# A new order of the four engines' work in the local attention layer of an eight-layer kernel

## The reference, cut to what matters

```
for i in range(DEPTH):                                   # 6
    q, k, v = heads(shift_tokens(x) @ Wqkv[i])
    q, k = rotary(l2norm(q) * qs), rotary(l2norm(k) * ksc)
    sim  = einsum(q_window, k_window_and_the_one_before) * 8
    attn = softmax(where(mask, -max, sim))
    x = merge(attn @ v) @ Wo[i] + x
    y = layernorm(shift_tokens(x)) @ W1 + b1             # feed-forward, inner 341, gelu
    x = (a * gelu(gate)) @ W2 + b2 + x
```

## Time and profile before

| | before |
|---|---|
| runs, median of 3 | 9571.57 us (9569.17 to 9572.25) |
| profiled execution | 9542.88 us, span 9541.1 us |
| PE busy | 7287.1 us (76%) |
| DVE busy | 6764.2 us (71%) |
| ACT, POOL busy | 3257.0 (34%), 3224.7 us (34%) |
| mean granted TensorE clock | 0.853 |

### The profile page before, as it was taken

One profiled execution on the slowest core, in us unless ns is written; L12 is line 12 of the kernel. 1 busy time (PEld: TensorE's weight loads), 2 busy tenths in 40 slices (PEclk: granted clock), 3 DMA queues, 4 the chain that ended last, 5 costly groups with the idle time before them and its releaser, 6 DMA issues. The chain is left out here.

```text
span 9541.1 us, 245537 instructions
## 1 busy us (share of the span) xinstructions
PE 7287.1 (76%) x92569; PEld 4453.7 (47%) x92569; DVE 6764.2 (71%) x15000; ACT 3257.0 (34%) x5970; POOL 3224.7 (34%) x3982
## 2 busy tenths in 40 slices
PE   4888888888874826656845768888888888888887
PEld 3666666666621212223223345545455545454554
DVE  7777777777758475765485557777777777777776
ACT  2222222222243313223413334444444444444444
POOL 1333333333300000210040035555555555555553
PEclk7888888888887867656865779999999999999999
DMA  0000000000000000000000031111111111111111
GB/s 18 1 1 1 1 1 1 1 1 1 1 5 1 15 0 0 0 0 1 0 0 1 1 120 54 53 53 54 48 56 51 54 51 51 56 51 56 51 56 57
DMA packets 156976, 243.21 MB, mean 25 GB/s; under 512 B 21617, under 2 KB 136849, under 8 KB 150161
## 3 DMA queue, kind: packets, MB, share of 16 engines
q1 hardware_dynamic: 155920, 228.84, 7.8%
HBM read 187.06 MB, written 13.66 MB: 21 GB/s over the span
## 5 line engine op out<-in xcount | busy, mean ns | idle before, releaser
L2751 POOL TENSOR_TENSOR big<-big 128x512 f32<-128x512 f32 x776 | 1040.1, 1373 | 278.4 <-DMA big<-norms 270.7
L2741 POOL TENSOR_TENSOR big<-big 128x512 f32<-128x512 f32 x388 | 494.7, 1275 | 1819.8 <-DVE big L2583 1819.8
L882 POOL TENSOR_TENSOR big<-big 128x128 f32<-128x128 f32 x1024 | 518.3, 506 | 1569.7 <-DVE big L820 1567.4
L604 ACT ACTIVATE big<-big 128x128 f32<-128x128 f32 x1024 | 316.8, 309 | 1902.0 <-DVE big L778 1876.8
L1856 POOL TENSOR_TENSOR small<-big 128x480 f32<-128x480 f32 (+14 forms) x240 | 220.9, 954 | 2187.2 <-ACT big L1614 1866.5
L2158 PE MATMUL banks<-hidden,big 128*128 128x256 f32 x3104 | 828.9, 401 | 111.8 <-DVE big L2583 41.1
L514 PE MATMUL banks<-big,constants_on_chip 128*128 128x128 f32 x2048 | 533.3, 347 | 409.8 <-DVE big L811 408.2
L337 PE MATMUL banks<-big,constants_on_chip 128*128 128x512 f32 (+15 forms) x1088 | 533.5, 644 | 355.2 <-DVE big L1747 191.3
L337 PE MATMUL banks<-big,weights_even 128*128 128x512 f32 (+5 forms) x1152 | 620.5, 692 | 235.0 <-DVE big L1137 45.1
L2222 PE MATMUL banks<-big,hidden 128*32 128x512 f32 x6144 | 770.5, 600 | 4.1 <-ACT big L2473 4.1
L2201 PEld LDWEIGHTS banks<-big 32*32 32x32 f32 x49152 | 535.2, 103 | 471.8 <-issue 471.1
(11 more groups left out here) (349 smaller groups left out, 15896.3 us busy)
## 6 DMA issues: line engine op xcount, KB each, us to landing
big<-norms SPq DMA_DIRECT2D x776, 128.0 KB, 2.9
big<-qk SPq DMA_DIRECT2D x50, 512.0 KB, 4.8
big<-vo SPq DMA_DIRECT2D x25, 1024.0 KB, 5.8
weights_odd<-ffn SPq DMA_DIRECT2D x25, 537.5 KB, 4.6
hidden<-big SPq DMA_DIRECT2D x171, 64.0 KB, 12.9
hidden<-big SPq DMA_DIRECT2D x25, 256.0 KB, 3.8
hidden<-big SPq DMA_DIRECT2D x25, 255.8 KB, 4.0
big<-pairs SPq DMA_DIRECT2D x6, 1024.0 KB, 10.4
```

The costliest lines, as they stand in the source:

```text
L882: nc.gpsimd.tensor_tensor(full(u["kS"][s % 2]), full(S), by(u["ko_c"]), ALU.mult).then_inc(*e.did(("kS", s)))
L2741: self.nc.gpsimd.tensor_tensor(dst, cos, sin, ALU.add).then_inc(*e.did(("turned_pair", f, name, g)))
L2751: self.nc.gpsimd.tensor_tensor(x, x, u["norms"][:, n, g].unsqueeze(1).broadcast_to([P, 2, QTOK]), ALU.mult).then_inc(*e.did(("scaled", f, ...
```

## The change

Each of the four compute engines gets a new list of steps for a phase. On TensorE, attend(f-1,1) stands behind four projections, two values, the masks and three score windows; the second masks and windows stand between the Q projections, the values and the rest of the phase; `turn_back` moves from the middle to near the end; both `mean`s move from f=0 to f=1. On ScalarE and VectorE `exps` and `normalise` of the second half go to the next phase, behind its first square and first rotation; `exit` runs the last of them. The Gelu table is loaded once in a phase that needs it. GpSimd adds Q0 before K3 and Q3 behind `keep_last`. `entry` clears the second probability buffer and five value slots in place of `probT`, the former behind the last store to DRAM. The number of matmuls, of products and of DMAs in a turn is the same. SyncE's program is not edited.

```diff
@@ -2226,10 +2226,9 @@
     def attend(self, q, jj):
         e, pe, u = self.e, self.pe, self.u
+        pe.wait_ge(*e.after("turned", q, jj))
         if e.layer == "local":
-            kw = {"back": 1} if jj and q == QUARTERS - 1 else {}
-            pe.wait_ge(*e.after("turned", q, jj, **kw))
-            pe.wait_ge(*e.after("kept", q, jj, 3, **kw))
+            pe.wait_ge(*e.after("kept", q, jj, 3, **({"back": 1} if jj and q == QUARTERS - 1 else {})))
             if jj == 0:
                 pe.wait_ge(*e.after("added", q))
...
@@ -2361,6 +2359,10 @@
             nc.vector.tensor_copy(u["folded"][d % 2][:, c * TILE:(c + 1) * TILE], core.bank[3 + c]).then_inc(
                 *e.did(("fold", d, c)))
         e.name_last("folded", d, "vector")
+    for k in range(2 * (SUBS * QUARTERS) - 5, 2 * (SUBS * QUARTERS)):
+        nc.vector.memset(u["slots"][k % SLOTS], 0.0).then_inc(*e.did())
+    dve.wait_ge(*e.after("stored", DEPTH - 1))
+    nc.vector.memset(u["prob"][1].rearrange("p c k -> p (c k)"), 0.0).then_inc(*e.did())
...
@@ -2382,46 +2384,51 @@
     t = LocalTensor(core, e)
     with e.turns("turn", TURNS):
         for f in range(QUARTERS):
-            for g in range(3):
-                t.project(f, "K", g)
-            t.attend((f - 1) % QUARTERS, 1)
-            t.project(f, "K", 3)
+            t.project(f, "K", 0)
+            t.project(f, "K", 1)
             t.value(f, 0, 0)
             t.value(f, 0, 1)
+            t.project(f, "K", 2)
+            t.project(f, "K", 3)
+            t.score_masks(f, 0)
+            t.score(f, 0, 0)
+            t.score(f, 0, 1)
+            t.score(f, 0, 2)
+            t.attend((f - 1) % QUARTERS, 1)
+            if f == 1:
+                t.mean(0)
+            t.score(f, 0, 3)
             t.sums(f, "K")
             t.project(f, "Q", 0)
-            t.score_masks(f, 0)
-            t.score(f, 0, 0)
+            t.value(f, 0, 2)
             t.project(f, "Q", 1)
-            t.score(f, 0, 1)
-            t.turn_back(f)
             t.project(f, "Q", 2)
-            t.score(f, 0, 2)
+            t.value(f, 0, 3)
+            t.score_masks(f, 1)
+            t.score(f, 1, 0)
             t.project(f, "Q", 3)
-            t.score(f, 0, 3)
+            t.value(f, 1, 0)
             t.sums(f, "Q")
-            t.value(f, 0, 2)
-            t.value(f, 0, 3)
+            t.score(f, 1, 1)
+            t.value(f, 1, 1)
+            if f == 1:
+                t.mean(1)
+            t.value(f, 1, 2)
             if f == 1:
                 t.variance(0)
-                t.variance(1)
-            if f == 3:
-                for win in range(4):
-                    t.value(f, 1, win)
+            t.score(f, 1, 2)
             if f >= 2:
                 t.up(f - 2, 0)
-            for win in range(4):
-                if f < 3:
-                    t.value(f, 1, win)
-                if win == 0:
-                    t.score_masks(f, 1)
-                t.score(f, 1, win)
-                if f >= 2 and win in (0, 3):
-                    t.up(f - 2, 1 if win == 0 else 2)
+            t.value(f, 1, 3)
+            if f >= 2:
+                t.up(f - 2, 1)
+            t.turn_back(f)
+            t.score(f, 1, 3)
+            if f >= 2:
+                t.up(f - 2, 2)
+            if f == 1:
+                t.variance(1)
             t.attend(f, 0)
-            if f == 0:
-                t.mean(0)
-                t.mean(1)
             if f >= 2:
                 t.down(f - 2)
     e.leave()
@@ -2457,7 +2464,8 @@
     def exps(self, f, jj):
         e, act = self.e, self.act
-        act.wait_ge(*e.after("lowered", f, jj))
+        if e.layer == "local":
+            act.wait_ge(*e.after("lowered", f, jj, **({"back": 1} if jj and f == QUARTERS - 1 else {})))
...
@@ -2519,36 +2523,43 @@
     core.nc.scalar.preload_act_table_set(LN_EXP)
     with e.turns("turn", TURNS):
         for f in range(QUARTERS):
-            for g in range(GROUPS):
-                a.square(f, "K", g)
+            a.square(f, "K", 0)
+            a.exps((f - 1) % QUARTERS, 1)
+            a.square(f, "K", 1)
+            a.square(f, "K", 2)
+            a.square(f, "K", 3)
             a.keep_value(f, 0, 0)
+            a.inverse(f, "K")
+            a.attention(f)
             a.keep_value(f, 0, 1)
             a.square(f, "Q", 0)
-            a.attention(f)
-            a.inverse(f, "K")
+            a.keep_value(f, 0, 2)
+            a.square(f, "Q", 1)
+            a.square(f, "Q", 2)
+            a.keep_value(f, 0, 3)
+            a.square(f, "Q", 3)
+            a.exps(f, 0)
+            a.keep_value(f, 1, 0)
             if f == 1:
                 a.ffn_squares(0)
-                a.ffn_squares(1)
-            for g in range(1, GROUPS):
-                a.square(f, "Q", g)
-            a.keep_value(f, 0, 2)
-            a.keep_value(f, 0, 3)
             a.inverse(f, "Q")
+            a.keep_value(f, 1, 1)
+            if f >= 2:
+                core.nc.scalar.preload_act_table(ACT.Gelu)
             if f == 1:
                 a.ffn_inverse(0)
+            a.keep_value(f, 1, 2)
+            if f == 1:
+                a.ffn_squares(1)
+            if f >= 2:
+                a.gelu(f - 2, 0)
+            a.keep_value(f, 1, 3)
+            if f == 1:
                 a.ffn_inverse(1)
-            if f == 3:
-                for win in range(4):
-                    a.keep_value(f, 1, win)
-            a.exps(f, 0)
             if f >= 2:
-                a.gelus(f - 2, range(1))
-            if f < 3:
-                for win in range(4):
-                    a.keep_value(f, 1, win)
-            if f >= 2:
-                a.gelus(f - 2, range(1, 3))
-            a.exps(f, 1)
+                a.gelu(f - 2, 1)
+                a.gelu(f - 2, 2)
+                core.nc.scalar.preload_act_table_set(LN_EXP)
...
@@ -2620,11 +2631,9 @@
         self.nc.vector.tensor_tensor(p, p, total.unsqueeze(2).broadcast_to([P, HEADS, 2 * WIN]), ALU.mult).then_inc(
             *e.did())
         self.chain()
-        if jj:
-            dve.wait_ge(*e.after("attended", (f - 1) % QUARTERS, 1))
-        else:
-            pf, kw = earlier(f)
-            dve.wait_ge(*e.after("attended", pf, 0, **kw))
+        if e.layer == "local":
+            pf, kw = earlier(f if jj == 0 else (f + 1) % QUARTERS)
+            dve.wait_ge(*e.after("attended", pf if jj == 0 else (f - 1) % QUARTERS, jj, **kw))
         self.nc.vector.transpose(u["probT"][jj].rearrange("p c w q -> p (c w q)").bitcast(U32),
                                  p.rearrange("p c k -> p (c k)").bitcast(U32)).then_inc(*e.did(("turned", f, jj)))
-            for name in NAMES:
-                for g in range(GROUPS):
-                    v.rope(f, name, g)
-                v.guard(f, name)
+            v.rope(f, "K", 0)
+            v.normalise((f - 1) % QUARTERS, 1)
+            v.rope(f, "K", 1)
+            v.rope(f, "K", 2)
+            v.rope(f, "K", 3)
+            if f == 1:
+                v.centre(0)
+            v.guard(f, "K")
             v.lower(f, 0)
-            v.add(f, (turn % BATCH) * SEQ + (f - 1) * QTOK if f else old + 3 * QTOK)
-            if f == 1:
-                v.norm(0)
+            v.rope(f, "Q", 0)
+            v.rope(f, "Q", 1)
+            v.rope(f, "Q", 2)
+            v.guard(f, "Q")
+            v.rope(f, "Q", 3)
+            v.normalise(f, 0)
             if f >= 2:
                 v.gate(f - 2, 0)
-            v.normalise(f, 0)
+                v.gate(f - 2, 1)
+            if f == 1:
+                v.centre(1)
+                v.norm(0)
+            v.add(f, (turn % BATCH) * SEQ + (f - 1) * QTOK if f else old + 3 * QTOK)
+            if f >= 2:
+                v.gate(f - 2, 2)
+            v.lower(f, 1)
             if f == 1:
                 v.norm(1)
             if f >= 2:
-                v.gate(f - 2, 1)
-                v.gate(f - 2, 2)
-            v.lower(f, 1)
-            if f == 0:
-                v.centre(0)
-                v.centre(1)
-            if f >= 2:
                 v.ffn_add(f - 2, old)
-            v.normalise(f, 1)
...
-            for name in NAMES:
-                for g in range(GROUPS):
-                    p.add(f, name, g)
+            p.add(f, "K", 0)
+            p.add(f, "K", 1)
+            p.add(f, "K", 2)
+            p.add(f, "Q", 0)
+            p.add(f, "K", 3)
+            p.add(f, "Q", 1)
+            p.add(f, "Q", 2)
             p.keep_last(f)
-            for name in NAMES:
-                for g in range(GROUPS):
-                    p.scale(f, name, g)
+            p.add(f, "Q", 3)
+            p.scale(f, "K", 0)
+            p.scale(f, "K", 1)
+            p.scale(f, "K", 2)
+            p.scale(f, "K", 3)
+            p.scale(f, "Q", 0)
+            p.scale(f, "Q", 1)
+            p.scale(f, "Q", 2)
+            p.scale(f, "Q", 3)
```

(24 more changed lines are left out.)

## The result

| | median | runs | ratio to before, 95% |
|---|---|---|---|
| before | 9570.37 us | 4, 9553.28 to 9572.25 | |
| changed kernel | 9355.72 us | 4, 9342.44 to 9364.65 | 0.9778 [0.9762, 0.9795] |

The change saves 215 us. The forecast was 419, to 9153; the time is also outside the range, 16 us above its upper end. Half of the gain is missing, and the question is where it went.

What follows compares the result with a forecast made beforehand. Bound by a chain (scores, lower, Exp, normalise, attend) whose consumer comes too early in TensorE's program. Work 137.4, waits 4.4 and supply 1.2 make a turn of 143.0 us against 160.6: gain 419, so 9153 us, range 9040 to 9340.

Steps and rivals of the forecast that it cites:

- instruction supply: TensorE's dense runs of score windows and attend: stops for late instructions, taken as 0.3 us a phase, 1.2 a turn.
- the pessimistic bound: Upper bound of the forecast: waits doubled and instruction stops of 1.0 us a phase, turn 150.2 us, time 9325 us.
- Rival B: TensorE's dense runs starve of instructions; 6 stops of 3.3 us a turn eat the gain, 8 give 9757; chance 4%.
- attend(f,0) for normalise and add: TensorE's wait before attend(f,0) for VectorE: 1.1 us in f=0, about 1.2 in f=1, 0 in f=2 and 3.
- masks for GpSimd: TensorE's masks wait for GpSimd's last scaling of the phase before: 1.1 us in f=1, otherwise 0.
- bank ring: K0 of the next turn takes the last down's bank and waits for ffn_add: 1.0 us a turn, as before.
- TensorE's work: TensorE's busy time in a turn: 139.4 us less 2.0 for pieces of low clock, 137.4.
- Second softmax a phase later: Before attend(f-1,1): probabilities ready 1.0 us before TensorE asks, so most of the 11.7 us a turn of waiting goes.
- First softmax: Before attend(f,0): VectorE normalises and adds by 28.4 us into the phase, TensorE arrives at 27.3, so it waits.
- GpSimd before the masks: Start of f=1: GpSimd's scaling ends at 36.2 us, masks stand at 36.05; 11 in hand before, now none.
- Gelu tables: ScalarE: one pair of Gelu table loads saved is worth 0, as it is busy at most 21.2 of 45 us.
- Clock: TensorE in the loop: with no idle above 1.2 us, low-clock pieces go, 2.0 us a turn; granted clock 0.99 or more.

Runs made afterwards that it cites:

- e5: The kernel before, with the 1 MB load of value weights in f=3 held until the scores of its second half are done: 9522.5 us.
- e1: The changed kernel, with projections and values put between the score windows in TensorE's first half of a phase: 9220.76 us.
- e2: The changed kernel, with GpSimd waiting for VectorE's product of the first softmax before it scales K: 9327.88 us.
- e3: The changed kernel with the edits of e1 and e2 together: 9236.47 us.
- e7: e3 plus first value of f=0 ahead of K0, turn_back ahead of the second masks, the add between the rotations of Q1 and Q2: 9298.73 us.
- e8: e1 with only the first value of f=0 moved ahead of K0: 9219.55 us.
- e9: e1 with turn_back before the second masks and VectorE's add between the rotations of Q1 and Q2: 9227.27 us.

## Why the prediction was wrong, step by step

**The step that failed is the instruction supply:** "A starved run costs 3.0 at most, none 0; I take 0.3 a phase." It measured 7.0 / 4 = 1.75 a phase. Behind it stood "I read the stop as instructions that came late behind that load", which e5 shows to be one third true, and the choice of the value "nearer to 0" because single windows beside nothing large "show 0.8 each and no such stop". A single window is 128 instructions between long matmuls; it says nothing about 254 and more in a row. Nor was the kernel before free of stops there: in f=0, behind three windows with a value between each, the fourth stops after 25 matmuls for 0.37 us (8047.65), and such a stop, of 0.5 on the mean, comes in 16 of the 19 turns from 6000 to 9000 us. The earlier trace rows had the right evidence: TensorE stopped after 182 matmuls, fewer than the new order puts together in every phase. These are 3 x 64 + 64 + 64 = 320, not 256: the prediction's count leaves out attend or a window, though its 5 us hold all five steps. Even the pessimistic bound, 1.0 a phase, was too low. Rival B named this mechanism and asked for 3.3 us at 6 stops a turn to lose the gain: the stops were six, at 7.0 / 6 = 1.2 each. The other terms alone would not have missed: e1, where the stops are 0.6 a turn, takes 9220.76 us, inside the stated range.

The turn, us, by the terms of the forecast:

| term | forecast | measured |
|---|---|---|
| instruction supply | 1.2 | 7.0 |
| attend(f,0) for normalise and add | 2.3 | 74.2 / 20.9 = 3.5 |
| masks for GpSimd | 1.1 | 0 |
| bank ring | 1.0 | 22.0 / 20.9 = 1.0 |
| variance for ScalarE; K3 for a rotation; attend(f-1,1) | 0 | 0.7; 0.6; 0.3 |
| TensorE's work | 137.4 | 2924.31 / 3200 x 152.9 = 139.7 |
| sum | 143.0 | 152.8 of 152.9 |

The last row but one is from the window of the loop of after:

```profile
6000.00:9200.00 3200.00, 2924.31 (x65675) 1649.89 (x65674) 2569.26 (x4606) 1328.54 (x2263) 1824.87 (x1402) 0.98 0.19 56
```

- *Second softmax a phase later:* right. Attend waits 11.7 less 3.8 = 7.9 less a turn, nearly all in front of attend(f,0), as said.
- *First softmax:* right in kind, 1.2 short. e2 shows the 1.1 of it: GpSimd's scaling beside the product. The prediction weighed that collision only for the time of the scaling, not for the product that it holds up. The Trainium skill ("SBUF — State Buffer", section "SBUF: two separate sides") calls the shared port pair an exclusive lock; 1.22 against 2.34 us, and 1.225 again once GpSimd waits, agree with it, and it speaks of both sides.
- *GpSimd before the masks:* 0, not 1.1, and not by the stops: those of f=0 (2.6 us) stand in front of the K sums and delay scaling and masks alike. In the turn shown the scaling ends at 8098.56 and the masks of f=1 come at 8101.00, so 2.4 were in hand, and in e1, almost without stops and with the masks two steps earlier, still 0.8. The "none in hand" was wrong because TensorE came later than forecast: attend(f,0) of f=0 begins 33.0 into the phase, not 28.4 (2.6 of the difference are the stops), and takes 3.4, not 1.9. Where the scaling begins later and attend is faster, no time is left: the masks wait 2.6 a turn in e3 and 5.7 in e7.
- *Bank ring and Gelu tables:* right, 1.0 and 0.
- *Clock:* the granted clock in the loop rose only from 0.97 to 0.98, not to 0.99, and TensorE's busy time did not fall: 2613.75 / 3000 x 160.6 = 139.9 before, 139.7 after. The idle times that were to go stayed, 2.35 us in f=0 and 1.24 in f=1, and attend behind them is still long:

```profile
8091.99 3.47 PE L2239 MATMUL banks<-big 128*32 128x128 f32 x56 [2.35 <-DVE big L2646]
```

  The mechanism was right where the idle does go: e2 shows 1.2 of the 2.0 a turn (139.7 to 138.5). In e1, with a clock of 0.99, the busy time is 2848.83 / 3000 x 146.8 = 139.4. There attend takes 343.87 / 3000 x 146.8 = 16.8 a turn, in after 356.34 / 3000 x 152.9 = 18.2, but scores and values take 0.9 and 0.8 more. And in the changed kernel the two means, which now stand apart, take 1.05 each (8106.70 to 8107.75), where both together took 1.82 before (8050.67 to 8052.49). Why steps that alternate cost more busy time is open.

Together: +5.8 (supply) + 1.2 - 1.1 + 0.7 + 0.6 + 0.3 + 2.3 (work) = 9.8 of the 9.9 missing. Also open: whether a stop is longer where the loop has just branched back. e8's 0.75 before the first value of a turn may be that; no run was made for it.

## What to carry to other kernels

Count instructions, not only microseconds: where small matmuls, each with its weight load, run on for hundreds of instructions (here the first stop came 266 to 488 instructions into a run), compare their rate (here 160 a us) with the supply (here 256 in 3.9 us), and put long matmuls between them; the mean rate over a loop is no guide. An "issue" stop inside a group of identical instructions is evidence of that, and a packet of the instruction queue that lands just before the engine goes on is stronger (here 1.2 to 1.6 us before, every time). A busy DMA beside it is not yet its cause: move the transfer before you blame it. When the longest wait goes, price the chains with nothing in hand, and where two engines slow each other price the delay of both; here e8 and e9 each shortened the wait they aimed at and gave nothing. And look at the clock behind a wait: in e2 it gave more than the wait.

## What was unexpected in the hardware

In a dense run TensorE's instructions came at one block of 256 in some 3.9 us even where the DMA engines were idle between two packets (a share of 0.00 in the windows above): the packet itself takes 1.2 of them, TensorE goes on 1.3 after it has landed, and the next packet starts 1.3 after that (8027.63 to 8028.97). The next phase of after, f=0, shows it again: its stops end at 8069.09 and 8073.04, 3.95 apart, with 127 matmuls and 127 weight loads between them. And a VectorE product of 128x1024 that starts with GpSimd's scaling takes 2.34 us, alone 1.22.
